# A transposed context by DMA in first attention, and the expert picks on GpSimd

## The reference

```python
def _L0_xattn_ref(x, context, Wq, Wk, Wv, Wo, bo):      # 8 heads of 64
    q, k, v = heads(x @ Wq), heads(context @ Wk), heads(context @ Wv)
    attn = softmax(einsum('bhsd,bhld->bhsl', q, k) * 64 ** -0.5)
    return merge(einsum('bhsl,bhld->bhsd', attn, v)) @ Wo + bo

def _L0_ffn_ref(x, gate_query, log_temp, w1, b1, w2, b2):
    affinity = _sinkhorn(einsum('bnd,ed->ben', x, gate_query) / exp(log_temp))
    gates, idx = top_k(affinity, CAP)                     # CAP = 32
    expert_in = take_along_axis(x[:, None], idx[..., None], axis=2)
    ...                                                   # an MLP for each of 16 experts, scattered back

x = x + tanh(g_xattn[0]) * _L0_xattn_ref(layernorm(x), ctx, ...)
x = x + tanh(g_ffn[0])   * _L0_ffn_ref(layernorm(x), ...)
x = x + tanh(g_xattn[1]) * _L1_xattn_ref(layernorm(x), ctx, ...)     # 16 heads
x = x + tanh(g_ffn[1])   * _L1_ffn_ref(layernorm(x), ...)
```

## Time and profile before

| | us |
|---|---|
| time before, median of 3 runs | 1878.68 (1876.93 to 1880.79) |
| the profiled execution's own time | 1875.75 |
| its span, first to last instruction | 1873.8 |
| PE busy | 1788.7 (95%) |
| DVE busy | 1621.6 (87%) |
| ACT busy | 1548.9 (83%) |
| POOL busy | 662.9 (35%) |
| keys of the first tile start, first attention | 21.82 |
| last of first attention's pipeline, about | 320 |
| experts' first tiles | 458 to 474 |

### The profile page before, as it was taken

How to read it: one execution, slowest core, us unless ns; L and a number is a source line. 1 busy time by engine, 2 the same in 40 slices (tenths; PEclk the granted TensorE clock), 3 DMA queues, 4 the chain that set the end, 5 groups by cost and what they waited for, 6 DMA issues and landing times. The chain is left out here.

```text
span 1873.8 us, 72646 instructions
## 1 busy us (share of the span) xinstructions
PE 1788.7 (95%) x28635; PEld 1313.7 (70%) x28635; DVE 1621.6 (87%) x3645; ACT 1548.9 (83%) x2773; POOL 662.9 (35%) x918
## 2 busy tenths in 40 slices
PE   6999998896999999999999999989999999999798
PEld 4787776542577777777777777767777777777587
DVE  5999998599799898989898988778999999988754
ACT  5999997475999999999999999867888888888543
POOL 3788887432000000000000000005666666655564
PEclk9999999898999999999999999999999999999899
DMA  7645444487000000000000001005665555533233
GB/s 178 138 95 100 97 95 89 152 317 262 15 13 15 13 15 13 13 13 12 16 10 18 11 15 51 2 15 126 162 160 150 155 145 154 147 72 70 68 116 121
DMA packets 312953, 160.66 MB, mean 86 GB/s; under 512 B 236558, under 2 KB 295862, under 8 KB 312374
## 3 DMA queue, kind: packets, MB, share of 16 engines
q1 hardware_dynamic: 312278, 157.95, 32.1%
q10 hardware_dynamic: 480, 0.05, 0.0%
HBM read 62.33 MB, written 36.83 MB: 53 GB/s over the span
## 5 line engine op out<-in xcount | busy, mean ns | idle before, releaser
L240 PEld LDWEIGHTS psE<-ew,h 128*128 128x128 f16 x6144 | 353.3, 98 | 33.8 <-DVE h L1803 5.0
L1803 DVE TENSOR_TENSOR h<-g,h 128x1024 f16<-128x1024 f32 x256 | 313.1, 1223 | 71.2 <-ACT h L1727 60.4
L240 PE MATMUL psE<-ew,h 128*128 128x128 f16 x6144 | 364.0, 219 | 2.6 <-DVE h L1803 2.6
L1722 ACT ACTIVATE g<-psH,eb1T 128x512 f32<-128x512 f32 x512 | 326.2, 679 | 19.5 <-PE psH L240 18.8
L815 POOL TENSOR_TENSOR Ph<-E,Ph 128x512 f16<-128x512 f32 x192 | 222.0, 1156 | 234.7 <-ACT Ph L769 234.7
L1876 POOL MEMSET rbias<- 64x384 f32 x1 | 0.4, 412 | 799.7 <-POOLq L133 799.7
L1727 ACT ACTIVATE h<-g 128x1024 f16<-128x1024 f32 x256 | 270.6, 1057 | 8.1
L721 ACT ACTIVATE vB<-psV 128x512 f16<-128x512 f32 x384 | 226.0, 589 | 50.4 <-PE psV L619 48.3
L842 DVE TENSOR_TENSOR vB<-psV,vB 128x512 f16<-128x512 f32 x384 | 248.3, 678 | 1.1 <-ACT vB L721 1.0
L619 PE MATMUL psV<-shared 96*64 96x512 f16 x1536 | 210.4, 380 | 1.5 <-DVE vB L842 1.5
L821 POOL TENSOR_TENSOR E<-E,rden 128x512 f32<-128x512 f32 x192 | 199.6, 1040 | 15.6 <-DVE rden L853 14.8
(11 more groups left out here) (313 smaller groups left out, 3387.9 us busy)
## 6 DMA issues: line engine op xcount, KB each, us to landing
keys_ahead<-shared SPq DMA_DIRECT2D x52, 512.0 KB, 4.9
shared<-keys_ahead SPq DMA_DIRECT2D x52, 512.0 KB, 3.6
rawe<-in_L_ffn_w_dram SPq DMA_DIRECT2D x32, 256.0 KB, 3.2
wb<-rw SPq DMA_DIRECT2D x64, 128.0 KB, 2.0
idx<-places SPq DMA_DIRECT2D x110, 64.0 KB, 2.6
out_dram<-x SPq DMA_DIRECT2D x7, 512.0 KB, 3.2
context_T<-shared SPq DMA_DIRECT2D x64, 48.0 KB, 2.4
PT<-Ph SPq DMA_TRANSPOSE x192, 2.8
```

Source lines behind the costliest of these rows:

```text
L240: last = e.matmul(to, a, b, start=start and n == 0, stop=stop and n == 2, **flags)
L1722: e.activation(g32[:, ft, :], psH[:, ft, :], ACT.Gelu_apprx_tanh, bias=b1T[:, a.expert(1) * FT + ft:a.expert(1) * FT + ft + 1]).then_inc(s ...
L1803: e.tensor_tensor(h[:, 1 - par, 1, 2 * q:2 * q + 2, :], g32[:, 2 * q:2 * q + 2, :], h[:, 1 - par, 0, 2 * q:2 * q + 2, :], ALU.subtract)\
```

## The change

In first attention, TensorE no longer transposes the context, and ScalarE no longer copies it out of PSUM. SyncE issues a DMA transpose of `cc` (128 partitions x 256 fp16 values, two blocks of 128 x 128, channels 96 to 127 being zero) straight into the ring of `cT`, for tile j+1 at the head of its body j and for tile 0 ahead of body 0. It waits there for GpSimd's low half (`clo`) and for the ring slot. TensorE's keys and SyncE's store to `context_T` wait for that DMA's semaphore (`ctx0` to `ctx3`) in place of ScalarE's (`ct`), and ScalarE waits for the transpose of tile j-1 before it overwrites its half of `cc`.

In `run_experts`, GpSimd makes all nine picks at once, ahead of use, into a part of `h` that is free then; VectorE makes none.

```diff
     cT1 = shared[0:DC, 64 * D:64 * D + 8 * P].rearrange("p (r h t) -> p r h t", r=4, h=2)
+    cT0 = shared[:, 64 * D:64 * D + 8 * P].rearrange("p (r h t) -> p r h t", r=4, h=2)
...
-            psC = psXC[:, P:2 * P].bitcast(F16).rearrange("p (k t) -> p k t", k=2)
...
                 def _(e):                                   # sync
                     def body(j):
                         a, a2, nx = Unit(j, 0), Unit(j, 2), Unit(j, -1)
+                        if first and nx.on:
+                            transpose_context(e, nx)
...
                         if a.opens and first:
-                            wait(e, s["ct"], a.t)
+                            wait(e, s[f"ctx{a.ring}"], ring(a.t, a.ring), 16)
...
+                    def transpose_context(e, a):
+                        wait(e, s["clo"], a.t)
+                        wait(e, s["Vb"], a.j - RING)
+                        wait(e, s[f"stored{a.ring}"], ring(a.t, a.ring) - 1, 16)
+                        e.dma_start_transpose(cT0[:, a.ring], cc[:, a.tp].rearrange("p h k -> p (h k)"))\
+                         .then_inc(s[f"ctx{a.ring}"], 16)
...
+                    if first:
+                        e.wait_ge(s["cc_pad"], 1)
+                        transpose_context(e, Unit(Step(None, 0, -1), -1))
...
                             if a.opens:                     # tensor
-                                if first:
-                                    wait(e, s["ct"], a.t)
-                                else:
-                                    wait(e, s[f"ctx{a.ring}"], ring(a.t, a.ring), 16)
+                                wait(e, s[f"ctx{a.ring}"], ring(a.t, a.ring), 16)
...
-                        if first and nx.on:
-                            for hl in range(2):
-                                for m in range(2):
-                                    last = e.transpose(psC[half(m), hl, :], cc[:, nx.tp, hl, half(m)], ident16[:])
-                            last.then_inc(s["C"], 1)
...
                         if first and nx.on:                 # scalar
-                            wait(e, s["C"], nx.t - 2)
+                            if a1.on:
+                                wait(e, s[f"ctx{a1.ring}"], ring(a1.t, a1.ring), 16)
                             e.activation(cc[:, nx.tp, 0, 0:DC], tile_of(nx.t, ctx32), ACT.Copy).then_inc(s["chi"], 1)
...
-                        if first and nx.on:
-                            wait(e, s["C"], nx.t)
-                            wait(e, s["Vb"], nx.j - RING)
-                            wait(e, s[f"stored{nx.ring}"], ring(nx.t, nx.ring) - 1, 16)
-                            e.activation(cT[:, nx.ring], psC[0:DC], ACT.Copy).then_inc(s["ct"], 1)
...
+                @block.gpsimd                               # run_experts
+                def _(e):
+                    for k in range(GT + 1):
+                        e.tensor_copy(pick[:, k].rearrange("p (b n) -> p b n", n=N),
+                                      ident16[:].rearrange("p (q t) -> p q t", q=2)[:, :, k:k + 1]
+                                      .broadcast_to([P, 2, N])).then_inc(s["pick"], 1)
...
-                    first_pick(0)
                     first_select(0)
-                    first_pick(1)
                     for k in range(GT):
                         first_select(k + 1)
                         if k + 2 <= GT:
-                            first_pick(k + 2)
+                            first_norm(k + 2)
                         first_rows(k)
```

More of the change, by code:

```diff
@@ L643, in tokens @@
                                 wait(e, s["ln"], nx.t)
-                                wait(e, s["ct" if first else "xt"], nx.t - 1)
+                                wait(e, s["xt"], nx.t - 1)
                                 for m in range(2):
@@ L701, in _ @@
                     if first:
-                        e.wait_ge(s["cc_pad"], 1)
                         pipeline(e, body, -1, U + 4, 8, U - 1, 4)
@@ L1477, in run_experts @@
             xn = sb(c, "xne", [P, 2, 2, D], F16)
-            pick = sb(c, "pick", [P, 2, P], F16)
             rows16 = idx16
@@ L1486, in run_experts @@
             h = sb(c, "h", [P, 2, 2, FT, ROWS], F16)
+            pick = h[:, 1, 1].rearrange("p k r -> p (k r)")[:, 0:(GT + 1) * P].rearrange("p (k t) -> p k t", t=P)
             put = sb(c, "put", [P, 2, RT, P], F16)
@@ L1588, in _, with batch_rows @@
                 def _(e):
-                    def batch_rows(par):
-                        e.matmul(psR[:], pick[:, par, :], idx16[:], start=True, stop=True).then_inc(s["R"], 1)
+                    def batch_rows(k):
+                        e.matmul(psR[:], pick[:, k, :], idx16[:], start=True, stop=True).then_inc(s["R"], 1)
                     def take_early(k, hl):
@@ L1614, in _ @@
                         wait(e, s["sel"], t)
-                        batch_rows((k + 1) % 2)
+                        batch_rows(k + 1)
                         for hl in range(2):
@@ L1735, in _ @@
                                  scale=column_of(tile0, rstd))
+                @block.gpsimd
[4 more added lines that the diff above has]
+                                      .broadcast_to([P, 2, N])).then_inc(s["pick"], 1)
                 @block.vector
                 def _(e):
-                    def queue_pick(t, par):
-                        wait(e, s["R"], t - 2)
-                        e.tensor_copy(pick[:, par].rearrange("p (b n) -> p b n", n=N),
-                                      ident16[:].rearrange("p (q t) -> p q t", q=2)[:, :, bass.ds(t.value, 1)]
-                                      .broadcast_to([P, 2, N])).then_inc(s["pick"], 1)
                     def queue_tile(t, par):
@@ L1774, in low_rows, with first_norm @@
                          .then_inc(s["g_0"], 1)
-                    def first_pick(k):
-                        queue_pick(Step(None, 0, k), k % 2)
+                    def first_norm(k):
                         if k == GT:
```

## The result

The changed kernel takes 1885.54 us (median of 7 runs, 1884.35 to 1887.29) against 1878.68 (7 runs, 1876.93 to 1882.29): a ratio of 1.0034, 95% interval 1.0024 to 1.0043. It is slower by a third of a per cent. The time lies in the range given (1873.5 to 1889) but outside the narrower one of the forecast itself (1875 to 1884), and the likeliest case, no change, was wrong by more than a measurement can miss.

What follows compares the result with a forecast made beforehand. TensorE's matmul stream was taken to bound first attention, ScalarE the experts' first tiles. Start +5.6, first units -0.8, TensorE -7.0, norms +1.5, load phase +0.7, picks 0 gave 0.0: 1875.8 us, 1878.7 on the median, range 1873.5 to 1889.

Steps and rivals of the forecast that it cites:

- the forecast itself: Whole kernel: the main forecast, 1875.8 us, or 1878.7 on the median, its own range 1875 to 1884; chance 0.55.
- the likeliest case, no change: Whole kernel: a time within 3.8 us, about 0.2%, of before; chance 0.46.
- The start: Tile 0's transpose waits behind SyncE's loads, so its keys move from 21.82 to 27.4: +5.6 us, bounds 5.0 and 7.5.
- The period: Steady first attention: TensorE loses 0.12 us per unit, 4.51 to 4.39, over 58 units: 7.0 us off.
- The landing: Steady first attention: the small transpose lands in 2.4 us, bounds 2.0 and 3.1, ready 0.6 us ahead of the keys.
- The load phase: Bodies 2 to 9, with large loads: transposes land 0.4 us late in two or three bodies, +0.7 us, range 0 to 3.
- a transpose's issue of at most 1.24 us ahead of them costs nothing: SyncE's queue: `PT` and expert weights behind the new transpose are needed two units later, so its issue delays nothing.
- The first units: First four units: ScalarE's chain sets the pace and loses its 0.26 us copy, -0.8 us, bounds 0 and 1.0.
- The norms: Three norms inside the full pipeline: VectorE's extra work loses 0.5 us of the gain each, +1.5 us, range 0 to 2.9.
- The picks: Experts' first tiles: ScalarE stays the bound, so moving picks to GpSimd is worth 0, range -0.2 to +0.4 us.
- The sum: Whole kernel: +5.6 - 0.8 - 7.0 + 1.5 + 0.7 + 0 = 0.0 us.
- the DMA closes the loop: Rival, first attention: at L (landing time) 3.6 us the period is 4.70, 1895 us; at 3.3, 1886.5 us; chance 0.17.

Runs made afterwards that it cites:

- the last version: Changed kernel with first two transposes early, one load per body in bodies 2 to 21, gate query late, norm stage moved: 1874.97 us (0.9984), again 1874.83 (0.9978).
- after: The changed kernel as made, against the kernel before: 1885.54 us, ratio 1.0034; its profiled execution took 1887.29 us.
- the context alone: The kernel before with only the attention's DMA transpose of the context, picks left on VectorE: 1883.19 us, ratio 1.0034.
- the control: The kernel before with the last version's spread loads, late gate query and moved norm stage, without the DMA transpose: 1877.88 us, ratio 0.9995.

## Why the prediction was right or wrong

- **The start, +5.6, keys near 27.4: right.** 27.61 and 27.36 in two traces. The 0.9 us for the transpose's data and receipt stood in no row, so that part of the hit was luck. Moving the transposes ahead of the loads brought the keys to 21.20, so the cause was the queue, as argued. The two transposes leave SyncE in 2.59 us together.
- **The period, 4.39: right.** It is 4.40, and VectorE's idle time before the scores 0.31, forecast 0.30. The distance between starts (0.12), not the transposes' own 0.29, was the right price.
- **The landing, 2.4: right.** 2.3, with 0.7 us to spare where 0.6 was worked out. The Trainium skill, VectorE: DVE Perf Modes (section The three transpose paths), gives 1309 ns for a 128 x 128 transpose by DMA, by which two would take 2.6 us as an estimate; the traces show 2.3. Its preference for TensorE (section Rules for kernel authors) held for this change as it was made, and no longer once the queue's order was changed (the last version).
- **The load phase, +0.7 (0 to 3): wrong, and the largest miss.** The term took 3.6 us to land, 0.4 late, in two or three bodies, and a period of 4.39 in the rest. Measured against eight periods less 0.11 each, it is 6.4 + 0.9 = 7.3 us in the trace of after and 2.4 + 0.9 = 3.3 in that of the context alone. Two things failed. The landing grew to 4.3 in the median of 70 to 82 and to 5.1 in the worst unit, though a larger landing stood in the rows (4.5 for `PT`, 5.3 at most). And "a transpose's issue of at most 1.24 us ahead of them costs nothing" holds for who stands behind it in the steady part, but nobody's row was added up for the load phase: there SyncE's issues come to 4.9 and 5.8 us in a body, more than a period, and the transpose goes out 2.4 us after its data are ready. SyncE was not in the list of engines whose share was asked for. A premise was wrong too: of the units from 4 on, counted as 58 at TensorE's pace, units 4 to 6 take 4.29, 7.78 and 6.14 us in before, TensorE waiting 3.07 for VectorE behind its first norm. There after and the context alone are 0.7 and 0.9 us faster, although tile 4's keys wait 1.2 and 2.0 for the DMA. The loss stands in units 7 to 11: 29.7 and 26.0 us against 22.6.
- **The first units, -0.8 (0 to -1.0): wrong.** Tiles 0 to 3 took 13.22 and 12.46 against 12.91: between -0.45 and +0.31 in two traces, with nothing of the gain sure. Tile 1's keys come 4.79 to 4.87 after tile 0's in both kernels, and the copy of 0.26 that left ScalarE didn't shorten that. The fourth unit is slower by 1.2 and 1.9, by its wait for the DMA; that is counted in the load phase.
- **The norms, +1.5 (0 to 2.9): in the range, and half of it by another cause.** From tile 11 to tile 61 the gain was 2.9 of a possible 50 x 0.11 = 5.5, so 2.6 was lost. 1.3 of it fits the argument, in the units beside the norms' operations (12 to 15, 26 to 31, 42 to 47 but for 46): units 14, 15, 30 and 31 take 4.85, 4.67, 4.85 and 4.69 us, as in before (4.82, 4.69, 4.82, 4.68), and VectorE waits for nobody in 14 and 15 of the changed kernel. Unit 46 alone is 6.00 - 4.90 + 0.11 = 1.2, by small operations of VectorE that met GpSimd's, and the forecast had no term for how long an operation takes beside another engine. Unit 20's DMA wait is 0.4 and unit 35 costs 0.3; six units (24, 36, 40, 48, 52, 56) gave 0.7 more than 0.11 each.
- **The last two units: not in the sum.** +0.8, with waits of 0.37 and 0.32 for the DMA. Before took 4.51 and 4.29 there.
- **The picks, 0: right**, shown by the run with them alone.
- **The sum**: with the load phase at its measured 3.3 to 7.3 in place of 0.7, the first units near 0, the tail at 0.8 and the steady loss at 2.6 in place of 1.5, it is +6.1 to +10.1 in place of 0.0 (5.8 + 3.3 or 7.3 - 6.4 + 2.6 + 0.8), and the median moved by 6.9. The rival "the DMA closes the loop" named 1886.5 us, close to the measured time, but for a wait in every unit; a steady period of 4.40 rules it out. The right number would have come from the wrong mechanism.

## What to carry to other kernels

When a transfer replaces work on an engine, add up the issuing queue's own time per period in every phase, as for any engine: a queue with 4.9 to 5.8 us of issues in a period of 4.4 delays what is needed next, although the steady part has room. Put what the first tile waits for ahead of bulk loads that are wanted later, and price each move with a control in which the old kernel gets it too: here the moves turned +0.34% into -0.16 and -0.22% in two measurements, where the control's 0.05% is within noise. And read one phase in more than one trace before a difference of a few us is believed.

## What the hardware showed that was not expected

- The issue of a DMA transpose on SyncE hardly depends on its size: 1.19 us in the median for two blocks (L579, 64 of them; first row below), 1.24 for eight. The store of the same 48 KB takes 0.50.

```profile
L579 SPq DMA_TRANSPOSE shared<-cc x64: 1167/1187/2467, 24.9 to 319.0; - x64
L556 SPq DMA_DIRECT2D context_T<-shared x64: 415/502/935, 27.6 to 323.9; - x64
```

- A VectorE operation of 0.17 us took 0.90 and 1.16 when GpSimd was in a two-input operation of 1.16, and ended within 0.03 us of it. Moving that stage away from body 44 gave 1.0 us net over the two units. VectorE's sum of rows ran beside the same GpSimd operation at its usual length, so not all of its operations are held. The held ones read two tensors from SBUF and the sum one; that this decides it wasn't tried.

```profile
239.94 0.68 DVE L850 TENSOR_REDUCE den<-E 128x8 f32<-128x512 f32 x1
239.97 1.16 POOL L814 TENSOR_TENSOR Ph<-E,Ph 128x512 f16<-128x512 f32 x1 [1.10 <-ACT Ph L773]
```

- The stage between first attention and the experts took 148.7 to 154.3 us for the same code, with a granted clock of 0.50 in one and 0.70 in another execution's window of 335 to 345 us; above 149.5 were only kernels with the DMA transpose, seven of their ten traces. What decides this stays open.
